# A fused transformer kernel, first phase: the feed-forward input's transposes go to another PSUM bank, and four small steps change places on TensorE and ScalarE

## What is computed

```python
x = x + attn_a(layernorm(x))      # 16 heads of 8 dims, rotary, q and k normalised per head,
                                  # softmax over all 256 keys
x = x + ffn(layernorm(x))         # the feed-forward block, below
x = x + attn_b(layernorm(x))      # windowed attention and a memory that is updated by gradients
x = x + ffn(layernorm(x))

def ffn(x):                       # per sequence
    x_prev = x shifted by one token (zeros first)
    xr = mu_r * x + (1 - mu_r) * x_prev
    xk = mu_k * x + (1 - mu_k) * x_prev
    r = sigmoid(xr @ W_r.T);  k = xk @ W_k.T
    return r * (square(relu(k)) @ W_v.T)
```

## Time and profile before

| | |
|---|---|
| median of 3 runs | 1362.33 us (1361.65 to 1364.27) |
| profiled execution | 1363.17 us, of which the span of the trace is 1361.3 us |
| first phase, alone on the chip | to about 600 us of the span; the second phase's set-up is woven into its last steps, and the rest (attention b, last feed-forward) follows to 1361.3 us |
| PE busy over the span | 1287.7 us, 95% |
| DVE, ACT, POOL busy | 82%, 66%, 37% |
| 300 to 400 us (steady steps of the first phase) | PE 95.50 us of 100, DVE 90.67, ACT 85.88, POOL 66.98; granted TensorE clock 1.00 |

### The profile page before, as it was taken

The page is one execution under the profiler, slowest core; times in us unless marked ns, Lnnn a source line. Parts: engine busy times, 40 slices in busy tenths (PEclk is TensorE's granted clock), DMA queues, the critical chain, the costliest instruction groups (busy, mean ns, idle before and its releaser), DMA issues.

```text
span 1361.3 us, 32944 instructions
## 1 busy us (share of the span) xinstructions
PE 1287.7 (95%) x10587; PEld 856.0 (63%) x10587; DVE 1111.8 (82%) x2790; ACT 900.9 (66%) x2504; POOL 503.9 (37%) x816
## 2 busy tenths in 40 slices
PE   7889999999999999888999999999999998999996
PEld 5445555555555555544666666666666665888885
DVE  4789999899999999876888888888888875778786
ACT  2278888888888888875565565556656653565553
POOL 4446666666666666532111111111111100332322
PEclk9899999999999999999999999999999999999997
DMA  2322322223333323210101010000000001232220
GB/s 69 91 77 79 78 78 74 78 81 81 85 92 103 100 76 84 68 42 17 34 26 32 25 53 27 30 25 28 28 28 25 21 17 43 79 86 82 86 85 28
DMA packets 102110, 79.69 MB, mean 59 GB/s; under 512 B 13797, under 2 KB 95270, under 8 KB 101942
## 3 DMA queue, kind: packets, MB, share of 16 engines
q1 hardware_dynamic: 100964, 77.05, 20.1%
q10 hardware_dynamic: 978, 0.54, 0.2%
HBM read 49.76 MB, written 27.79 MB: 57 GB/s over the span
## 4 chain that ended last, share of the span: by engine, by line
PE 49%; DVE 1%; issue 1%; ACT 1%; POOL 0%; POOLq 0%; DVEq 0%; ACTq 0%
PE b_psZ L1430 4%; PE b_psD L1351 4%; PE b_psZ L1362 4%; PE b_g L1414 4%; PE d_psO L1974 4%; PE b_g L1401 4%; PE d_psH L1966 4%; PE b_psM L1463 2%; PE b_psR L1407 2%; PE b_psL L1392 2%; PE b_psR L1423 2%; PE b_psD L1453 2%; PE b_psM L1475 1%; PE d_psG L1992 1%; PE d_psV L2005 1%
## 5 line engine op out<-in xcount | busy, mean ns | idle before, releaser
L811 DVE TENSOR_REDUCE a_MX<-a_psS 128x4 f32<-128x1024 f32 x248 | 303.4, 1224 | 47.3 <-PE a_psS L313 47.3
L607 ACT ACTIVATE a_PT<-a_psE 128x512 f32<-128x512 f32 x504 | 274.9, 604 | 59.6 <-PE a_psE L330 56.2
L1831 POOL TENSOR_TENSOR b_SWB<-b_b2col,b_SW 128x128 f32<-128x128 f32 x65 | 38.7, 595 | 346.3 <-ACT b_SW L1546 346.3
L344 PE MATMUL a_psV<-a_PT,a_VX 128*32 128x256 f32 x2048 | 137.0, 385 | 0.2 <-ACT a_PT L607 0.2
L1565 ACT ACTIVATE b_TH<-b_psZ 128x512 f32<-128x512 f32 x65 | 38.8, 597 | 128.8 <-PE b_psZ L1362 124.4
L313 PE MATMUL a_psS<-a_KS,a_QS 48*128 48x256 f16 x992 | 97.8, 275 | 23.5 <-DVE a_MX L811 20.6
L330 PE MATMUL a_psE<-a_QS,a_KS 50*128 50x256 bf16 x1008 | 97.5, 270 | 3.1 <-ACT a_PT L607 3.1
L313 PEld LDWEIGHTS a_psS<-a_KS,a_QS 48*128 48x128 bf16 x992 | 29.2, 94 | 104.6 <-DVE a_MX L811 65.6
L1585 ACT ACTIVATE b_PR<-b_psL,b_mx 128x128 f32<-128x128 f32 x260 | 92.9, 368 | 0.9
L344 PEld LDWEIGHTS a_psV<-a_PT,a_VX 128*32 128x32 f32 x2048 | 53.4, 109 | 50.5 <-issue 27.5
L1713 DVE SCALAR_TENSOR_TENSOR b_HH<-b_TH,b_psZ 128x512 f32<-128x512 f32 x65 | 44.7, 688 | 44.0 <-ACT b_TH L1565 43.9
(11 more groups left out here) (309 smaller groups left out, 3407.0 us busy)
## 6 DMA issues: line engine op xcount, KB each, us to landing
a_KS<-kparts SPq DMA_DIRECT2D x63, 192.0 KB
a_QS<-qparts SPq DMA_DIRECT2D x126, 96.0 KB
qparts<-a_QP SPq DMA_DIRECT2D x64, 96.0 KB, 2.2
a_X<-x_in SPq DMA_DIRECT2D x32, 128.0 KB, 2.2
kparts<-a_KP SPq DMA_DIRECT2D x64, 64.0 KB, 2.1
x<-a_X SPq DMA_DIRECT2D x32, 128.0 KB, 1.9
b_X<-x SPq DMA_DIRECT2D x32, 128.0 KB, 2.2
zT<-b_XT SPq DMA_DIRECT2D x32, 128.0 KB, 1.7
```

The costliest lines, as they stand in the source:

```text
L344: mm = nc.tensor.matmul(psV[32 * h:32 * h + 32, 0:T], VX[:, b % UV, kt, at:at + 32], PT[:, gg, kt, h, :], start=(gg == 0 and kt == 0), sto ...
L607: nc.scalar.activation(PT[:, g % 2, :, h + s, :], shifted_bank(b, p, s), ACT.Exp).then_inc(S["exp"], 1)
L811: nc.vector.reduce_max(MX[:, b % 2, :].rearrange("q (s n) -> q s n", s=2)[:, :, 2 * p:2 * p + 2], score_banks(b, p)[:], AX.X).then_inc(S[" ...
```

## The change

It does four things. (1) `fz_t` of the sequences b < 26 writes `psA` instead of `psC`; it waits for `square` and `centred` of sequence b + 6 instead of `on` of b + 1, ACT's copies read `psA`, and the K product now waits for all four copies (`fzT`). `on_t` waits for the copies of the sequence before only where these still use `psC` (b - 1 = 26 to 29). (2) On PE, `on_t` goes from slot 5 to the end of slot 4, ahead of the scores of slot 5; in slot 5, `z_t` and the K product stand between `scores` and `shifted`, and the R product stays behind `shifted` (`ffn_kr` is cut into `ffn_k` and `ffn_r`). (3) On ACT, the copies of part 0 go from slot 4 to slot 3, ahead of the slot 4 exponentials; `ot(c-4, 0)`, `on_t` and `z_t` go ahead of the slot 5 exponentials. (4) In DVE's source the call of `x1` is written a few lines earlier in the same slot; the order of DVE's instructions is unchanged, and so are POOL's and SP's. Counts of instructions are the same on every engine.

```diff
         def on_t(b):
             wait(pe, "on", b)
-            if b < B - 1:
+            if B - 6 <= b - 1 < B - 2:
                 wait(pe, "fzT", b - 1, per=4)
...
         def fz_t(b):
             wait(pe, "fz", b)
-            if b == B - 1:
+            if b < B - 6:
+                wait(pe, "square", b + 6)
+                wait(pe, "centred", b + 6)
+            elif b == B - 1:
                 wait(pe, "x1", b)
...
-                to = psE[0][:, 0, t * P:(t + 1) * P] if b == B - 2 else psC[:, t * P:(t + 1) * P]
+                to = (psE[0][:, 0, :] if b == B - 2 else psC if b >= B - 6 else psA)[:, t * P:(t + 1) * P]
...
-        def ffn_kr(b):
+        def ffn_k(b):
...
             wait(pe, "centred", b + 6)
+            wait(pe, "fzT", b, per=4)
...
             nc.tensor.matmul(psA[:, 0:T], wk_t[:], FX[:, 1, :], start=True, stop=True)
+
+        def ffn_r(b):
             wait(pe, "mixed", b, per=2)
...
+                if p == 5:
+                    if on(c + 1):
+                        z_t(c + 1)
+                    if on(c - 6):
+                        ffn_k(c - 6)
                 if on(c - 4):
                     shifted(c - 4, p)
...
                     if on(c - 4):
                         pv(c - 4, 1)
-                if p == 5:
                     if on(c - 5):
                         on_t(c - 5)
-                    if on(c + 1):
-                        z_t(c + 1)
+                if p == 5:
                     if on(c - 6):
-                        ffn_kr(c - 6)
+                        ffn_r(c - 6)
...
+            src = psA if b < B - 6 else psC
+            nc.scalar.activation(FC[:, part, :], src[:, 0:T], ACT.Copy, scale=vecs[:, 4 + part:5 + part]).then_inc(S["fzT"], 1)
...
         def body(c):
             for p in range(NP):
+                if p == 5:
+                    if on(c - 4):
+                        ot(c - 4, 0)
+                    if on(c - 5):
+                        on_t(c - 5)
+                    if on(c + 1):
+                        z_t(c + 1)
                 if on(c - 4):
                     exps(c - 4, p)
...
                 if p == 3:
                     if 0 <= c - 6 < B - 4:
                         fz_t(c - 6, 1)
-                if p == 4:
-                    if 0 <= c - 6 < B - 4:
                         fz_t(c - 6, 0)
-                    if on(c - 4):
-                        ot(c - 4, 0)
                 if p == 5:
-                    if on(c - 5):
-                        on_t(c - 5)
-                    if on(c + 1):
-                        z_t(c + 1)
                     if on(c):
                         spread(c)
```

More of the change, by code:

```diff
@@ L571, in closing @@
             yield B + 4, 1
-            ffn_kr(B - 2)
+            ffn_k(B - 2)
+            ffn_r(B - 2)
             on_t(B - 1)
@@ L579, in closing @@
             yield B + 4, 4
-            ffn_kr(B - 1)
+            ffn_k(B - 1)
+            ffn_r(B - 1)
             yield B + 4, 5
@@ L679, in fz_t @@
             wait(act, "mixed", b - 1, per=2)
-            nc.scalar.activation(FC[:, part, :], psC[:, 0:T], ACT.Copy, scale=vecs[:, 4 + part:5 + part]).then_inc(S["fzT"], 1)
-            nc.scalar.activation(FP[:, part, 1:T], psC[:, 0:T - 1], ACT.Copy, scale=past[:, part:part + 1]).then_inc(S["fzT"], 1)
+            src = psA if b < B - 6 else psC
+            nc.scalar.activation(FC[:, part, :], src[:, 0:T], ACT.Copy, scale=vecs[:, 4 + part:5 + part]).then_inc(S["fzT"], 1)
+            nc.scalar.activation(FP[:, part, 1:T], src[:, 0:T - 1], ACT.Copy, scale=past[:, part:part + 1]).then_inc(S["fzT"], 1)
         def ffn_kr(b):
@@ L971, in body @@
                         normed(c)
+                    if on(c - 5):
+                        x1(c - 5)
                 if p == 0:
@@ L981, in body @@
                         fz_copies(c - 6)
-                if p == 6:
-                    if on(c - 5):
-                        x1(c - 5)
                 if p == 7:
```

## The result

The changed kernel takes 1369.48 us (median of 5 runs, 1367.91 to 1372.62); the kernel before, run beside it, 1362.33 us. The ratio is 1.0052, 95% interval 1.0038 to 1.0066: slower by 0.5%, about 7 us, where 1364.3 us and a range up to 1368.0 had been forecast. The profiled execution took 1369.32 us with a span of 1367.5 us, 6.2 us more than the span before. The medians are 7.15 us apart, 1 us more than the two traces; single runs of either kernel spread over some 5 us.

The account below looks back on a forecast made before the run. PE was the fullest engine, but ACT, without idle time, was taken to bound the new order. 26 steps at 0.05 us (1.3 us) plus 0.7 us for the last steps made 2.0 us: 1362.33 to 1364.3 us, range 1359.0 to 1368.0.

Parts of the forecast that it names:

- The wait that goes, and where the gain is given back: Output transposes' 0.35 us wait a step goes; PE's 0.56 us lead lost in some 0.6 us wait in slot 6.
- the new conditions of `fz_t` and of K: `fz_t`'s waits for slot 1 work cost nothing; K's wait for all copies, ending about 313.8, hidden before K at 314.47.
- What holds the exponentials: Slot 5's exponentials on ACT: held by ACT's own earlier work until 315.42, not by PE, ready at 315.32.
- ACT's own 315.42: hidden, with 0.10 us to spare: Slot 5: `shifted` at 314.90 lets ACT's pair start at 315.32, before ACT is free at 315.42; 0.10 us slack.
- The sign that I had named for this: ACT idle before its slot 5 pair would show the forecast wrong, the pair waiting for PE.
- Rival (2): Slot 5's ACT pair waits for PE's `shifted`, late behind Z's transposes and K: 4.6 us slower, 1366.9 us, chance 0.31.
- the ends: Steps 32 and 33 about -0.15 us each, 34 +0.70, 35 +0.28: together +0.7 us, bounds -0.5 and +1.5.
- ACT's walk: Summing ACT's rows from first copy: slot 5 pair from 315.42, ends 316.50 to 316.55; slot 6's `shifted` 316.56 to 316.61.
- The 0.05 us that a step was to lose: Slot 6's `shifted` later by +0.01 to +0.06 us a step, taken as +0.05; 26 steps make 1.3 us.
- Rival (3): Seven ACT neighbours before slot 5's pair pack 0.03 us closer each, 0.2 us a step: 1359.1 us, chance 0.08.
- (4): PE keeps its 0.56 us a step, ACT not being the bound: -14.6 + 0.7 us, 1348.4 us, chance 0.06.
- The page's price: ACT's copies to ONT and ZT at 0.31 us each, 0.61 both, against the trace's 0.56; sum would be 3.3 us.

## Why the prediction was wrong

**The wait that goes, and where the gain is given back: right.** The output transposes wait for nothing, DVE's wait before slot 6's row maximum is gone, and a new wait of PE before line 330 in slot 6 takes the place, released by ACT's exponentials; it is 0.34 us long (from 318.57 + 0.23 to 319.14) instead of some 0.6, since PE comes later than summed. Also right: the new conditions of `fz_t` and of K (13.9 us are all on line 330, none on 465 or 477), and POOL and the queues.

**What holds the exponentials: wrong.** The step of the prediction that failed is "ACT's own 315.42: hidden, with 0.10 us to spare". It had slot 5's exponent matmuls at 314.90, 3.15 us after the feed-forward transposes; they come at 3.40. The missing 0.25 us are three distances that I took from other neighbours. (1) The output transposes in slot 4 take 0.37 us to slot 5's scores, not the 0.23 us that two transposes take to another float32 matmul. I had read the 0.36 us between `fz_t` and the scores in the kernel before (311.75 in the earlier trace rows, then 312.11) as a wait for DVE, and that row can't tell, as the row maximum had ended 0.06 us before these scores:

```profile
310.83 1.22 DVE L811 TENSOR_REDUCE a_MX<-a_psS 128x4 f32<-128x1024 f32 x1 [0.18 <-PE a_psS L313]
```

(2) Z's transposes take 0.28 us to K, not 0.23. (3) K takes 0.53 us to the 16-bit group, not 0.43. So the pair waits for PE, 0.15 us beyond ACT's own work. The sign that I had named for this, ACT idle before the pair, doesn't show as a wait in the trace, since the row of the ZT copy lasts 0.42 us and so fills the time up to 318.00; the distance tells, 0.42 us from that copy to the pair instead of 0.26 with K behind. Rival (2) was the case, by its mechanism, its place and its point of decision. Its price was nearly right for the steady steps (0.05 + 0.10 us a step, 3.9 us, against 0.16 us on average, 4.12 us), and too small in all by the ends.

**ACT's walk: right, where it applies.** With K behind, the pair starts at 3.66 and PE's matmuls at 4.85, inside the sum. The 0.05 us that a step was to lose is nearly what this kernel loses (17.93 against 17.87). Rival (3) asked for ACT to be faster than its rows and (4) for PE not to be held by it, and neither shows in the changed kernel.

**The page's price.** The copies to ONT and ZT stood 0.28 us apart (317.30, 317.58), and with K behind they cost 0.54 us together (315.93 to 316.47), near the 0.56 us of the earlier trace rows and below the estimate of 0.31 us each worked out from the Trainium skill (ScalarE: Activation LUTs, What ACT_TABLE_LOAD costs), so the traces don't agree with it to that size. It is of no consequence in the changed kernel: taking both copies away from the pair changed no steady step.

**The ends: mis-sized or missed.** Steps 2 to 5 were not looked at. The two traces differ by 0.88 us there: 0.05 us is there before slot 5 of step 4, 0.22 us arises in slots 5 and 6 of that step, where Z's transposes now stand ahead of the exponent matmuls, and 0.61 us in slots 5 and 6 of step 5, where the ONT copy besides waits for Z's transposes (0.70 us idle on ACT). The lengths from one sequence's feed-forward transposes to the next tell the last steps, each by the slot 5 that lies in it:

| step | before | changed | difference | predicted |
|---|---|---|---|---|
| 31 | 15.64 | 15.71 | +0.07 | +0.05 |
| 32 | 15.71 | 15.90 | +0.19 | -0.15 |
| 33 | 15.07 | 15.26 | +0.19 | -0.15 |
| 34 | 15.89 | 16.38 | +0.49 | +0.70 |
| 35 | 12.11 | 12.40 | +0.29 | +0.28 |

Step 35 was right, and step 34 was 0.2 us too dear. Steps 32 and 33 had the wrong sign: the K product ahead of the exponent matmuls is what costs there too, for with K behind they take 15.49 and 14.77 us, less than before. Steps 32 to 35 together: +1.16 instead of +0.7 us.

**The terms.** The 26 steady steps, 31 among them: 4.12 us instead of 1.3. The first steps: 0.88 us, which had no term. Steps 32 to 35: 1.16 us instead of 0.7. The sum of 2.0 us became 6.2. My range ended at rival (2) with its price and 1.1 us more; the two uncertain terms, a slack of 0.10 us a step and the ends, were both on the slow side and had to be added.

## What to carry to other kernels

Work that is moved ahead of an instruction which releases another engine is no filler: price it on the path, by moving a copy of it to either side if in doubt (here 0.43 against 0.05 us a step). Take a distance from a row with the same neighbours on both sides, above all where groups of different data type alternate, and when a slack is smaller than the spread of such distances, forecast its rival. A wait that goes may uncover two more behind it (here the last copy and POOL's sum), so changes that are worthless or harmful alone can pay together: the bank move with the early copies costs 0.27 us a step, the whole order without K ahead and without the ONT and ZT copies ahead gains 0.12.

## What the runs showed of the hardware

All distances are from start to start, at a granted clock of 1.00. Two float32 transposes take 0.21 to 0.24 us to a following float32 matmul (0.27 to 0.28 right behind a 16-bit group) and 0.35 to 0.37 us to a following 16-bit group. K's two matmuls take 0.43 to 0.44 us between float32 matmuls, 0.53 us before a 16-bit group, and 0.53 to 0.54 us behind one with R after them. R's four take 0.54 us behind K. Between two 16-bit groups they take 0.64 us in the kernel with K twice ahead; in the changed kernel the scores behind R come after 0.67 us, but there DVE's row maximum holds them (317.30 + 1.22 = 318.52, scores at 318.57). So a change between the two kinds costs about 0.1 us of PE in these rows, with less behind a 16-bit group for the transposes, and the changed kernel has one change more each way in every step.

The weight loads say what goes with it. R in the kernel before, in the changed one, and in the one with the bank move alone (shown above, 314.85):

```profile
315.60 0.60 PEld L476 LDWEIGHTS a_psA<-a_wr_t,a_FX 128*128 128x128 f32 x4
```

```profile
317.90 0.52 PEld L482 LDWEIGHTS a_psA<-a_wr_t,a_FX 128*128 128x128 f32 x4 [0.21 <-issue]
```

Behind K the load starts 0.18 us ahead of R's first matmul (315.60, 315.78), and behind a 16-bit group together with it (317.90). With the bank move alone R stands behind K, but POOL holds its load, so that load and matmul start together again (314.85), and R takes the same 0.64 us without any change of kind. So the 0.1 us fits a weight load that doesn't run ahead of its matmul; why it doesn't behind the other kind isn't shown by any run.

PE restarts 0.05 to 0.06 us after ACT's last exponential ends, in all the kernels in which it waits.
